# L1 cross attention and L2 attention in a new order, and wide FFNs rounded by ScalarE to int16 and transposed by DMA

## The chip, the cores and the metric

The kernel runs on one core of one Trainium2 chip. The time is the device time of one execution in microseconds. One program computes a whole decoder stack of twelve sublayers for eight sequences.

## The reference, cut to what matters

`x` is [8, 256, 256]. Four layers follow one another, each with self attention, cross attention and an FFN, and after every sublayer comes `x = layernorm(x + sublayer(x))`. The change touches five of the twelve:

```python
# L1 cross attention: 16 heads of 16, context of 64 tokens
q = qdq(x) @ qdq(wq).T + bq        # qdq: s = max|row|/127, round(x/s) clipped to +-127, times s
attn = softmax(q @ k.T / 4)
out = qdq(attn @ v) @ qdq(wp).T + bp
# L1, L2, L3 FFN: 256 -> 1024 -> 256, ternary weights, activations rounded per token
xq = round(x * 127 / max|x|)       # L1F: x and hidden are first RMS-normed and multiplied by g
h = silu(xq @ w1.T) * (xq @ w2.T)  # L2F: with biases; L3F: 128 levels, h goes through a Walsh-Hadamard transform
out = quant(h) @ w3.T
# L2 attention: linear attention with decay, 16 heads of 16, chunks of 128
scores = (q @ k.T) * decay_mask    # per head and chunk
intra = scores @ v;  inter = (q * q_decay) @ kv
out = rms_norm(intra + inter) @ wo
```

## The kernel before, in words

Each sublayer is a function that opens one or more blocks. In a block every engine has a program of its own, and semaphores order them. The sublayers follow one another with a barrier between them. They are called L0A, L0X, L0F, L1A, L1X and so on (layer; A attention, X cross attention, F FFN), and the names of their tiles begin with that. `x` stays in SBUF as `X`, 128 rows by two tiles a sequence. `v(...)` issues a VectorE instruction and lets VectorE wait until it has finished, unless `free=True` is given. The weights of the next sublayer are loaded during the one before, by the queue of SP (`prefetch`). All matmuls on attention data are float32, those of the wide FFNs bfloat16 on whole numbers.

**L1X** (`sublayer_l1_cross`) takes a sequence in U = 4 steps u (two tiles of 128 rows, two groups of 8 heads). In a step TensorE makes `scores(u + 1)` (one matmul of 512 columns), `turn(u - 1)` (four transposes of the probabilities) and `values(u - 2)`; VectorE takes the maxima and differences (L1818, L1821), ScalarE the exponential (L1803) and the copy of the turned tile (L1797). The rest of a sequence hangs on the step's number r = u % 4. On VectorE: r = 0 the next sequence's input is quantized (`quantize_rows`: maximum, scale, reciprocal, two multiply-and-add-magic (L1625), two subtract-and-scale (L1627)); r = 1 the outputs of the sequence before are divided and quantized; r = 2 the queries get bias and scale (`vec_q`, L1648); r = 3 the residual, the statistics, a wait for GpSimd's power -1/2, and the scaling. On TensorE: r = 1 turns the quantized input, r = 2 turns the outputs and makes the next queries, r = 3 projects. The last sequence's projection has a block of its own (`last_rows`).

**The wide FFNs** (`sublayer_ternary_ffn`; L1F with norms, L2F with biases, L3F with the Hadamard transform) take 16 tiles of 128 rows, one a step s, in a software pipeline. VectorE in step s: `quantize_input(s)`, `quantize_hidden(s - 3)`, `norm(s - 4)`, the two halves of `gate_times_up(s - 1)`, in L3F `across_chunks(s - 1)` (six additions), and `scale_and_add(s)` (the maximum and scale of the hidden tile s - 2, the residual and statistics of tile s - 3). ScalarE: silu of the gates of tile s - 1, the copy of the turned hidden tile, the copy of the turned input, and last the multiplication by the reciprocal scale with the rounding constant added (L1430). TensorE: the gates of s - 1, eight transposes of the rounded hidden tile s - 3 (L1354), its down projection into the same bank, the transposes of the input s. In L3F eight transposes and eight matmuls of the transform stand between them.

**L2A** (`sublayer_l2_attn`) takes a sequence in U = 8 steps of two heads; the heads lie 32 rows apart in the array (`at`), and the output of `values` lies in 32 columns of it. In step u TensorE makes `scores(u + 1)` (four matmuls of 128 columns, all with the row group of u), `values(u - 2)`, and a piece of the work around it: r = 0 turns x, r = 1, 2 queries and keys, r = 2, 3 the output projection, r = 4 values, r = 5, 6, 7 turned pieces and the keys' product. VectorE multiplies the scores by the decay (`decay`, L2583) and rotates (L2351). The tile `sd` has three buffers.

**L0A** and **L0X** aren't changed, but they contain the same operations: L0A makes its scores by turns over two row groups (L492) and its values over four column groups (L520); L0X has DMA transposes issued by SP (L810) and a VectorE conversion from int16 to bfloat16 (L925).

## Time and profile before

| | us |
|---|---|
| three runs | 3930.85, 3927.05, 3930.51 |
| median | 3930.51 |
| the profiled execution, its own time | 3925.62 |
| its span, first to last instruction | 3923.8 |

Over the span TensorE is busy 3158.0 us (80%), VectorE 2699.9 (69%), ScalarE 1818.9 (46%), GpSimd 467.4 (12%). Such shares are a mean over twelve stages with different limits; which engine bounds a stage is read from a window of that stage. Busy time of TensorE also grows when its clock is granted at half speed, so the granted clock has to be read beside it.

### The profile page before, as it was taken

How to read it: one execution, taken by the hardware profiler on the slowest of the kernel's cores; microseconds unless marked ns; L12 is line 12 of the kernel's file. 1: busy time of each engine (PE TensorE's matmuls, PEld its weight loads, DVE VectorE, ACT ScalarE, POOL GpSimd, SP SyncE). 2: the span in 40 equal slices, each digit the busy share in tenths (PEclk: the TensorE clock that was granted, in tenths of full speed). 3: DMA queues.
4: the chain of work that ended last, by engine and by line, in shares of the span. 5: the costliest groups of instructions: out<-in, count | busy, mean ns of one | idle time of the engine just before them, and what ended most of it. 6: DMA issues, size and time to landing. Idle time of an engine off the chain costs nothing. (4 is left out here: it accounts for less than half of the span.)

```text
span 3923.8 us, 55642 instructions
## 1 busy us (share of the span) xinstructions
PE 3158.0 (80%) x17296; PEld 2305.3 (59%) x17296; DVE 2699.9 (69%) x8364; ACT 1818.9 (46%) x5598; POOL 467.4 (12%) x585
## 2 busy tenths in 40 slices
PE   7975555979999997765599974579999999999565
PEld 5653334747777776542277762247777777777354
DVE  4668885278788885668844468856666666666597
ACT  4547673145555552225411123346666666666243
POOL 0012110011111110111101110011111111111100
PEclk9995556989999998765599996689999999999588
DMA  1005554000000001000000012000000000000000
GB/s 58 1 24 95 102 103 129 1 14 1 1 1 1 1 1 41 1 31 1 16 1 1 1 45 105 1 11 1 1 1 1 1 1 1 1 1 1 33 1 22
DMA packets 141731, 83.68 MB, mean 21 GB/s; under 512 B 135424, under 2 KB 139648, under 8 KB 139776
## 3 DMA queue, kind: packets, MB, share of 16 engines
q1 hardware_dynamic: 141440, 80.14, 7.8%
q8 instruction: 142, 2.33, 0.2%
q14 instruction: 149, 1.22, 0.1%
HBM read 44.47 MB, written 2.10 MB: 12 GB/s over the span
## 5 line engine op out<-in xcount | busy, mean ns | idle before, releaser
L2219 DVE CUSTOM_DVE_ANT_0 L3A_masked<-ps,L3A_hidden,L3A_negrstd 128x128 f32<-128x128 f32 (+1 forms) x512 | 193.6, 416 | 321.9 <-PE ps L2110 232.7
L2168 ACT ACTIVATE L3A_probs<-L3A_masked,L3A_negmax 128x128 f32<-128x128 f32 (+1 forms) x512 | 228.7, 449 | 237.3 <-DVE L3A_negmax L2219 237.2
L336 PE MATMUL ps<-s_weights_b,s_XT 128*128 128x512 f32 (+1 forms) x640 | 299.6, 597 | 30.0 <-ACT L1A_qn L2026 8.3
L2138 PE MATMUL ps<-s_weights_b,L3A_OT 128*128 128x256 f32 x1024 | 264.2, 381 | 14.5 <-DVE s_R L2248 14.5
L336 PE MATMUL ps<-s_weights_b,s_Xc 128*128 128x512 f32 x512 | 243.6, 598 | 7.5 <-DVE L3A_rot L2083 3.3
L2091 POOL TENSOR_TENSOR L3A_rstd<-L3A_ve,s_mhalf 128x4 f32<-128x4 f32 x144 | 145.0, 1007 | 849.7 <-DVE L3A_ve L2051 849.7
L885 ACT ACTIVATE L0X_pf<-ps,L0X_bias,L0X_qscale 128x512 int16<-128x512 f32 x256 | 197.0, 777 | 90.8 <-DVE L0X_bias L918 90.2
L336 PEld LDWEIGHTS ps<-s_weights_b,s_XT 128*128 128x128 f32 x640 | 121.8, 209 | 121.7 <-issue 72.3
L2138 PEld LDWEIGHTS ps<-s_weights_b,L3A_OT 128*128 128x128 f32 x1024 | 175.1, 191 | 28.8 <-issue 15.6
L915 DVE TENSOR_REDUCE L0X_negmax<-ps 128x2 f32<-128x1024 f32 x128 | 156.1, 1220 | 35.5 <-PE ps L826 35.0
L2168 ACT ACTIVATE L1A_probs<-L1A_masked,L1A_negmax 128x128 f32<-128x128 f32 (+1 forms) x256 | 114.3, 447 | 120.2 <-DVE L1A_negmax L2219 117.5
L2016 ACT ACTIVATE s_oT<-ps 128x128 bf16<-128x128 f32 x576 | 150.8, 277 | 22.5 <-PE ps L336 22.5
L320 POOL TENSOR_TENSOR s_rs<-s_ve,s_mhalf 128x2 f32<-128x2 f32 x74 | 55.3, 747 | 874.2 <-DVE s_ve L264 874.2
L2110 PE MATMUL ps<-L3A_kT,L3A_qT 128*128 128x256 f32 x512 | 154.3, 383 | 0.0
L2127 PE MATMUL ps<-L3A_probsT,L3A_V 128*128 128x256 f32 x512 | 152.5, 380 | 0.0
L2091 POOL TENSOR_TENSOR L1A_rstd<-L1A_var,s_mhalf 128x4 f32<-128x4 f32 x80 | 82.5, 1031 | 562.1 <-DVE L1A_var L2046 562.1
L2138 PE MATMUL ps<-s_weights_b,L1A_OT 128*128 128x256 f32 x512 | 131.9, 380 | 8.9 <-DVE s_R L2248 8.9
L336 PE MATMUL ps<-s_XT,s_weights_a 128*128 128x256 f32 (+1 forms) x512 | 124.7, 397 | 12.5 <-ACT s_XT L205 5.4
L2127 PEld LDWEIGHTS ps<-L3A_probsT,L3A_V 128*128 128x128 f32 x512 | 89.1, 190 | 72.2 <-issue 72.1
L336 PEld LDWEIGHTS ps<-s_weights_b,s_Xc 128*128 128x128 f32 x512 | 87.4, 191 | 74.5 <-issue 63.0
L2003 ACT COPY L3A_qT<-ps 128x512 f32<-128x512 f32 x128 | 75.1, 587 | 117.9 <-PE ps L1987 117.9
L546 ACT ACTIVATE L0A_probs<-ps,L0A_negmax 128x128 f32<-128x128 f32 (+1 forms) x256 | 86.6, 422 | 90.8 <-DVE L0A_negmax L581 90.0
(512 smaller groups left out, 8650.6 us busy)
## 6 DMA issues: line engine op xcount, KB each, us to landing
s_weights_b<-w_L3A SPq DMA_DIRECT2D x1, 9984.0 KB, 27.0
s_weights_b<-w_L1A SPq DMA_DIRECT2D x1, 7936.0 KB, 21.4
s_weights_a<-w_L2F SPq DMA_DIRECT2D x1, 4224.0 KB, 12.3
s_weights_b<-w_L1F SPq DMA_DIRECT2D x1, 3840.0 KB, 11.9
s_weights_b<-w_L3F SPq DMA_DIRECT2D x1, 3136.0 KB, 11.1
s_weights_a<-w_L2A SPq DMA_DIRECT2D x1, 2898.0 KB, 9.8
s_weights_a<-w_L0F SPq DMA_DIRECT2D x1, 2176.0 KB, 9.0
s_X<-x SPq DMA_DIRECT2D x1, 2048.0 KB, 8.3
```

What stands on the lines that cost most here:

```text
L336: last = pe.matmul(out, lhs(k), rhs(k), start=(k == 0), stop=(k == n - 1))
L546: last = a.activation(pr[:, p % 4, x, cols], c.bank(2 * (p % 2) + x)[:, cols], ACT.Exp, bias=nmx[:, p % 4, j, x:x + 1])
L885: last = a.activation(pf[:, p % 3, x, :], c.bank(2 * (p % 3) + x), ACT.Exp, scale=qs[:, b % 2, at:at + 1], bias=nms[:, p % 4, x:x + 1], ac ...
L915: v(eng.tensor_reduce(nmx[:, p % 4, :], c.ps[:, 2 * (p % 3):2 * (p % 3) + 2, :], AX.X, ALU.max, negate=True))
L2003: a.copy(dst[:, 2 * b:2 * b + 2, :].rearrange("p h t -> p (h t)"), c.bank(2)).then_inc(side_taken, 1)
L2016: last = a.activation(squares[:, j, s * P:(s + 1) * P], c.bank(j)[:, s * P:(s + 1) * P], ACT.Square, accum_out=var[:, j, s:s + 1])
L2091: p.tensor_tensor(rstd[:, j, 4 * slot(g):4 * slot(g) + 4], src[:, j, :], c.mhalf[:, 0:4], ALU.pow).then_inc(pow_ready, 1)
L2110: pe.matmul(bank[:, P:3 * P], qT[:, g % 2, s, P:TOK], kT[:, i % 2, h // REP, :], start=True, stop=True).then_inc(scores_made, 1)
L2127: pe.matmul(c.bank(7)[:, 0:TOK], V[:, i % 2, 0, d], prT[:, u % 2, 0:TOK], start=True, stop=False)
L2138: last = pe.matmul(c.bank(3)[:, j * DM:(j + 1) * DM], OT[:, u % 4, j * P:(j + 1) * P], w["wo"][:, h, :], start=(h == 0 and j == 0), stop=( ...
L2168: last = a.activation(pr[:, u % 4, cols], ms[:, u % 2, cols], ACT.Exp, bias=nmx[:, h, j:j + 1], scale=-1.0, accum_out=sm[:, h, j:j + 1])
L2219: last = eng.tensor_tensor_reduce(out=ms[:, u % 2, cols], in0=s[:, cols], in1=hidden[:, P - j * P:2 * P], scale=-1.0 if gated else nrs[:, ...
```

## The change

**L1X.** Both roundings (of the inputs and of the outputs) go to ScalarE as two activations each: multiply and write int16, multiply again and write float32. VectorE keeps maximum, scale and reciprocal (`row_scales`). ScalarE also makes the queries' bias and scale. GpSimd adds the projection's bias to x. The inputs are rounded and turned a sequence ahead, outputs are turned at r = 3 and projected at r = 0 of the sequence after the next, the residual is at r = 2 and its scaling at r = 0 after that. The loop has two more rounds, and the block of the last projection goes.

**L2A.** Two heads make a pair; their scores are issued by turns, and so are their values; the pieces of other work stand between and after. `sd` has four buffers, and VectorE does two decays in a row.

**The wide FFNs.** ScalarE multiplies and writes int16, both for the inputs (`round_input`) and for the hidden tile. The hidden tile is transposed by a DMA from SP's queue, and then converted to bfloat16: in L1F and L2F by ScalarE, in L3F by VectorE (`clip_hidden`). TensorE's eight transposes and the copy out of PSUM go. VectorE's order within a step changes: `norm`, the gates, `quantize_input` (now one conversion), across, clip, `scale_input(s + 1)`, `scale_and_add`. The down projection is one step later (LAG = 4). In L1F the factor of the RMS norm is applied to the scales and not to the rows.

```diff
+    LAG = 4
...
+            @block.sync
+            def _(sp):
+                for t in range(NT):
+                    sp.wait_ge(hround_ready, t + 1)
+                    if t >= 2:
+                        sp.wait_ge(hiT_ready, t - 1)
+                    sp.dma_start_transpose(out=hqT[:, t % 2, :].rearrange("p (c q) -> p c q", q=P), in_=hq[:, t % 2, :]).then_inc(
+                        hq_turned[t % 2], 16)
...
-                for s in range(NT + 3):
+                for s in range(NT + LAG):
                     if 1 <= s <= NT:
                         gates(s - 1, 0)
                         gates(s - 1, 1)
                     if hadamard and 2 <= s < NT + 2:
                         turn_hidden(s - 2)
-                    if s >= 3:
-                        turn_quantized(s - 3)
                     if hadamard and 2 <= s < NT + 2:
                         transform(s - 2)
-                    if s >= 3:
-                        down(s - 3)
+                    if s >= LAG:
+                        down(s - LAG)
...
+                def round_input(t):
+                    a.wait_ge(xscale_ready, t + 1)
+                    if t >= 2:
+                        a.wait_ge(xi_ready, t - 1)
+                    for q in range(XQ):
+                        x = qx[:, q, :] if norms else row(t)
+                        last = a.activation(xq[:, t % 2, q, :], x, ACT.Copy, scale=rq[:, t, q:q + 1])
+                    last.then_inc(xround_ready, 1)
...
+                    if s < NT:
+                        round_input(s)
                     if 1 <= s <= NT and not biases:
                         silu(s - 1, 0)
...
-                    if s >= 3:
-                        a.wait_ge(hi_turned, s - 2)
-                        a.copy(hiT[:, (s - 3) % 2, :], c.bank(7, BF16)).then_inc(hiT_ready, 1)
...
+                    if s >= 3 and not hadamard:
+                        t = s - 3
+                        a.wait_ge(hq_turned[t % 2], 16 * (t // 2 + 1))
+                        if t >= 2:
+                            a.wait_ge(y_tile, t - 1)
+                        a.copy(hiT[:, t % 2, :], hqT[:, t % 2, :]).then_inc(hiT_ready, 1)
...
-                        a.activation(qh[:], x, ACT.Identity, bias=c.magic[:, 0:1],
-                                     scale=rc[:, s - 2, 2:3]).then_inc(hround_ready, 1)
+                        if s >= 4:
+                            a.wait_ge(hq_turned[s % 2], 16 * (s // 2 - 1))
+                        a.activation(hq[:, s % 2, :], x, ACT.Copy, scale=rq[:, s - 2, 2:3]).then_inc(hround_ready, 1)
...
+                def scale_input(t):
+
+                    last = XQ - 1
+                    if norms:
+                        if t:
+                            eng.wait_ge(xround_ready, t)
+                        for q in range(XQ):
+                            v(eng.tensor_tensor(qx[:, q, :], row(t), w["g1" if q == 0 else "g2"], ALU.mult), free=q < last)
+                        v(eng.tensor_reduce(am[:, t, 0:XQ], qx[:], AX.X, ALU.max, apply_absolute_value=True))
+                        eng.wait_ge(xrr_ready, t + 1)
+                        v(eng.tensor_scalar(am[:, t, 0:XQ], am[:, t, 0:XQ], rr[:, t, 0:1], least, ALU.mult, ALU.max))
+                        v(eng.tensor_scalar(am2[:, t, 0:XQ], am[:, t, 0:XQ], 1.0 / levels, None, ALU.mult))
+                    else:
+                        v(eng.tensor_reduce(am[:, t, 0:1], row(t), AX.X, ALU.max, apply_absolute_value=True))
+                        v(eng.tensor_scalar(am2[:, t, 0:XQ], am[:, t, 0:XQ], least, 1.0 / levels, ALU.max, ALU.mult))
+                    v(eng.reciprocal(rc[:, t, 0:XQ], am2[:, t, 0:XQ]), None if norms else xscale_ready, free=not norms)
+                    if norms:
+                        v(eng.tensor_scalar(rq[:, t, 0:XQ], rc[:, t, 0:XQ], rr[:, t, 0:1], None, ALU.mult), xscale_ready, free=True)
+                    b_ = am2[:, t, 0:XQ] if norms else am2[:, t, 0:1].to_broadcast([P, 2])
+                    v(eng.tensor_tensor(f[:, t, 0:2], b_, wsc[:, 0:2], ALU.mult))
...
+                    eng.wait_ge(xround_ready, t + 1)
...
+                    x = xq[:, t % 2].rearrange("p q d -> p (q d)")
+                    o = xi[:, t % 2].rearrange("p q d -> p (q d)")
+                    v(eng.tensor_scalar(o, x, levels - 1.0 if hadamard else levels, None, ALU.min), xi_ready, free=True)
...
+                def clip_hidden(t):
+                    eng.wait_ge(hq_turned[t % 2], 16 * (t // 2 + 1))
                     if t >= 2:
-                        eng.wait_ge(hi_turned, t - 1)
-                    whole(v, hi[:, t % 2, :], qh[:], hi_ready)
+                        eng.wait_ge(y_tile, t - 1)
+                    v(eng.tensor_scalar(hiT[:, t % 2, :], hqT[:, t % 2, :], levels - 1.0, None, ALU.min), hiT_ready, free=True)
...
-                for s in range(NT + 4):
+                scale_input(0)
+                for s in range(NT + LAG + 1):
                     if norms and 2 <= s < NT + 2:
                         hidden_mean(s - 2)
-                    if s < NT:
-                        quantize_input(s)
-                    if 3 <= s < NT + 3:
-                        quantize_hidden(s - 3)
-                    if s >= 4:
-                        norm(s - 4)
+                    if s > LAG:
+                        norm(s - LAG - 1)
+                    if norms and s + 1 < NT:
+                        input_mean(s + 1)
                     if 1 <= s <= NT:
                         for hf in range(NH):
                             gate_times_up(s - 1, hf)
-                        if hadamard:
-                            across_chunks(s - 1)
-                    if norms and s + 1 < NT:
-                        input_mean(s + 1)
+                    if s < NT:
+                        quantize_input(s)
+                    if hadamard and 1 <= s <= NT:
+                        across_chunks(s - 1)
+                    if hadamard and 3 <= s < NT + 3:
+                        clip_hidden(s - 3)
+                    if s + 1 < NT:
+                        scale_input(s + 1)
...
+        def row_scales(v, out, x, sem):
+
+            e = v.eng
+            v(e.tensor_reduce(am[:], x, AX.X, ALU.max, apply_absolute_value=True))
+            v(e.tensor_scalar(out[:, 0, :], am[:], 1.0 / 127.0, 1e-8, ALU.mult, ALU.max))
+            v(e.reciprocal(out[:, 1, :], out[:, 0, :]), sem, free=True)
+
+        def act_quantize(a, out, x, whole, scales, rounded, first, ready):
+
+            for k in range(TT):
+                a.activation(whole[:, k, :], x[:, k, :], ACT.Copy, scale=scales[:, 1, k:k + 1]).then_inc(rounded, 1)
+            for k in range(TT):
+                a.wait_ge(rounded, first + k + 1)
+                a.activation(out[:, k, :], whole[:, k, :], ACT.Copy, scale=scales[:, 0, k:k + 1]).then_inc(ready, 1)
...
+        def act_q(a, b, t=0):
+            a.wait_ge(q_made, t + 1)
             for ch in range(KC):
-                v(v.eng.tensor_scalar(qT[:, b, ch, :], c.bank(0)[:, ch * TOK:(ch + 1) * TOK], w["bq"][:, ch:ch + 1],
-                                      DH ** -0.5, ALU.add, ALU.mult), q_ready)
+                a.activation(qT[:, b, ch, :], c.bank(0)[:, ch * TOK:(ch + 1) * TOK], ACT.Identity, bias=bqs[:, ch:ch + 1],
+                             scale=DH ** -0.5).then_inc(q_ready, 1)
...
+                for u in range((NS + 2) * U):
                     b, r = u // U, u % U
                     if u + 1 < NS * U:
                         scores(u + 1)
                     if 1 <= u <= NS * U:
                         turn(u - 1)
-                    if u >= 2:
+                    if 2 <= u < NS * U + 2:
                         values(u - 2)
-                    if b == NS:
-                        continue
-                    if r == 1:
+                    if r == 0 and b + 1 < NS:
                         pe_turn_xq(pe, b)
-                    if r == 2:
-                        if b:
-                            pe.wait_ge(S.on_ready, TT * b)
-                        S.pe_turn_on(pe, 6)
+                    if r == 0 and b >= 2:
+                        project_outputs(b - 2)
+                    if r == 1 and b + 1 < NS:
                         pe_q(pe, b)
-                    if r == 3:
-                        S.pe_project_on(pe, wpT, 7, b)
+                    if r == 3 and 1 <= b <= NS:
+                        turn_outputs(b - 1)
...
+                for u in range((NS + 2) * U):
                     b, r = u // U, u % U
                     if u < NS * U:
                         a.wait_ge(diff_ready, u + 1)
                         a.activation(pr[:, u % 2, :], pr[:, u % 2, :], ACT.Exp).then_inc(exp_ready, 1)
-                    if u >= 1:
+                    if 1 <= u <= NS * U:
                         take(u - 1)
-                    if b < NS and r == 1:
+                    if r == 0 and b + 1 < NS:
+                        if b:
+                            a.wait_ge(q_made, b)
                         S.act_xT(a, t=b)
-                    if b < NS and r == 2:
-                        S.act_oT(a, 6, b)
+                    if r == 1 and b + 1 < NS:
+                        act_q(a, (b + 1) % 2, b)
+                    if r == 2 and 1 <= b <= NS:
+                        act_on(a, b - 1)
+                    if r == 3 and b + 2 < NS:
+                        act_xq(a, b + 2, b + 1)
+                    if r == 3 and 1 <= b <= NS:
+                        if b > 1:
+                            a.wait_ge(S.y_made, b - 1)
+                        S.act_oT(a, 6, b - 1)
...
+                def residual(i):
+                    eng.wait_ge(S.y_made, i + 1)
+                    eng.wait_ge(xb_ready, i + 1)
+                    v(eng.tensor_tensor(c.R[:], Xb[:], c.bank(7).rearrange("p (j d) -> p j d", j=TT), ALU.add), S.y_read)
+                    S.vec_norm_stats(v)
+
+                row_scales(v, xs, c.X[:, 2 * TT:3 * TT, :], x_scaled)
+                for u in range((NS + 2) * U + 1):
                     b, r = u // U, u % U
                     if u < NS * U:
                         differences(u)
-                    if b and r == 1:
+                    if r == 0 and b >= 3:
+                        S.vec_norm_scale(v, b - 2, b - 3)
+                    if r == 1 and 1 <= b <= NS:
                         outputs(b - 1)
-                    if b == NS:
-                        continue
-                    if r == 0:
-                        quantize_rows(v, Xq, c.X[:, bass.ds((b + 2) * TT, TT), :], xq_ready)
-                    if r == 2:
-                        vec_q(v, (b + 1) % 2, b)
-                    if r == 3:
-                        S.vec_add_y(v, b, 7, w["bp"], b)
-                        S.vec_norm_stats(v)
-                        S.vec_norm_scale(v, b, b)
+                    if r == 2 and b >= 2:
+                        residual(b - 2)
+                    if r == 3 and b + 2 < NS:
+                        eng.wait_ge(xq_ready, TT * (b + 1))
+                        row_scales(v, xs, c.X[:, (b + 3) * TT:(b + 4) * TT, :], x_scaled)
...
+                        g.tensor_tensor(Xb[:], c.X[:, (b - 1) * TT:b * TT, :], over(w["bp"], TT), ALU.add).then_inc(xb_ready, 1)
+                        S.pool_rstd(g, b - 2)
...
+                def scores(p):
+                    b = 2 * p // U
+                    if b and 2 * p % U == 0:
                         pe.wait_ge(turned_ready, 5 * b - 1)
-                    if u >= 2:
-                        pe.wait_ge(sd_ready, u - 1)
-                    at, chunks = heads(u)
-                    for x, ch in enumerate(chunks):
+                    if p:
+                        pe.wait_ge(sd_ready, 2 * p)
+                    for x in range(2):
                         for j in range(TT):
                             t = slice(j * P, (j + 1) * P)
-                            last = pe.matmul(c.bank(4 + u % 2)[:, x * TOK + j * P:x * TOK + (j + 1) * P], qT[at, b % 2, 1, ch, t],
-                                             qT[at, b % 2, 0, ch, t], start=True, stop=True)
-                    last.then_inc(scores_made, 1)
-
-                def values(u):
+                            for u in (2 * p, 2 * p + 1):
+                                at, chunks = heads(u)
+                                last = pe.matmul(c.bank(4 + u % 2)[:, x * TOK + j * P:x * TOK + (j + 1) * P], qT[at, b % 2, 1, chunks[x], t],
+                                                 qT[at, b % 2, 0, chunks[x], t], start=True, stop=True)
+                                if x == j == 1:
+                                    last.then_inc(scores_made, 1)
...
+                            for u in (2 * p, 2 * p + 1):
+                                at, _ = heads(u)
+                                d = slice(ch * P + at.start, ch * P + at.stop)
+                                last = pe.matmul(bank[at, x * TOK + j * P:x * TOK + (j + 1) * P], V[:, b % 2, j, d], sd[:, u % 4, x, j, :],
+                                                 start=False, stop=(x == j == 1))
+                                if x == j == 1:
+                                    last.then_inc(o_made, 1)
...
+                for p in range(NS * U // 2 + 1):
+                    b, r = 2 * p // U, 2 * p % U
+                    if b < NS:
+                        scores(p)
+                        side(b, r)
+                    if p:
+                        values(p - 1)
+                    if b < NS:
+                        side(b, r + 1)
...
-                    decay(u)
+                    if u % 2 == 0:
+                        decay(u)
+                        decay(u + 1)
```

## Rows read from the trace of the kernel before

**Rows 1.** Busy time by window: L1X, L2A, one tile of L1F.
```profile
core 0: us, PE busy (x) PEld busy (x) DVE busy (x) ACT busy (x) POOL busy (x), PEclk, DMA share, GB/s
...
1553.00:1748.00 195.00, 147.73 (x650) 111.08 (x648) 127.44 (x298) 44.47 (x81) 22.32 (x29) 0.75 0.00 1
...
1974.00:2256.00 282.00, 274.81 (x1724) 215.94 (x1722) 119.49 (x352) 48.22 (x96) 27.31 (x32) 0.96 0.00 1
...
1824.20:1834.84 10.64, 6.94 (x28) 3.36 (x28) 10.01 (x27) 5.43 (x9) 1.59 (x3) 0.50 0.00 0
```

**Rows 2.** Tile view of L1X_pr: the differences of the 32 steps.
```profile
L1821 DVE TENSOR_TENSOR L1X_pr<-ps,L1X_mx x32: 690/692/692, 1553.1 to 1730.0; 128x512 f32<-128x512 f32 x32
```

**Rows 3.** Timeline of L1X, TensorE: start, duration (us), idle before.
```profile
1644.24 2.07 PE L1745 MATMUL ps<-L1X_kd,L1X_qT 128*128 128x512 f32 x2 [4.15 <-DVE L1X_pr L1821]
...
1658.76 1.12 PE L1745 MATMUL ps<-L1X_kd,L1X_qT 128*128 128x512 f32 x2 [1.10 <-DVE L1X_qT L1648]
...
1660.97 1.97 PE L336 MATMUL ps<-L1X_wpT,s_oT 128*128 128x256 f32 x8
1662.78 1.02 PE L1745 MATMUL ps<-L1X_kd,L1X_qT 128*128 128x512 f32 x2
```

**Rows 4.** Timeline of L1X, VectorE.
```profile
1648.76 0.26 DVE L1829 RECIPROCAL L1X_ri<-ps 128x16 f32<-128x16 f32 x1 [0.82 <-PE ps L1766]
...
1651.52 0.62 DVE L1625 TENSOR_SCALAR L1X_tmp<-s_R,L1X_inv 128x256 f32<-128x256 f32 x2
...
1657.70 1.00 DVE L1648 TENSOR_SCALAR L1X_qT<-ps,s_weights_a 128x256 f32<-128x256 f32 x2 [3.46 <-PE ps L336]
```

**Rows 5.** Timeline of L2A, TensorE.
```profile
2101.02 1.15 PE L2493 MATMUL ps<-L2A_qT 32*128 32x128 f32 x8
2102.11 1.06 PE L2514 MATMUL ps<-L2A_sd,L2A_V 128*32 128x128 f32 x8
2103.10 1.09 PE L2384 MATMUL ps<-s_const,L2A_rp 128*128 128x128 f32 x8
```

**Rows 6.** Timeline of L0A, TensorE.
```profile
151.03 0.92 PE L492 MATMUL ps<-L0A_kT,L0A_qT 32*128 32x128 f32 x8
151.89 0.40 PE L496 MATMUL ps<-s_causal_bf,s_idb 128*128 128x128 bf16 x4
...
155.09 0.86 PE L520 MATMUL ps<-L0A_probsT,L0A_V 128*32 128x256 f32 x16
155.88 0.92 PE L492 MATMUL ps<-L0A_kT,L0A_qT 32*128 32x128 f32 x8
```

**Rows 7.** Tile views of the rounded hidden tiles of L1F, L2F, L3F (min/median/max ns).
```profile
L1298 DVE TENSOR_SCALAR L1F_hi<-L1F_qh x16: 693/694/705, 1791.9 to 1943.2; 128x1024 bf16<-128x1024 f32 x16
...
L1298 DVE TENSOR_SCALAR L2F_hi<-L2F_qh x16: 693/694/695, 2397.3 to 2557.2; 128x1024 bf16<-128x1024 f32 x16
...
L1298 DVE TENSOR_SCALAR L3F_hi<-L3F_qh x16: 693/694/696, 3743.0 to 3907.8; 128x1024 bf16<-128x1024 f32 x16
```

**Rows 8.** Timeline of one tile of L3F, VectorE.
```profile
3808.05 0.42 DVE L1455 TENSOR_REDUCE L3F_am<-s_X 128x1 f32<-128x256 f32 x1
...
3808.95 0.35 DVE L1461 TENSOR_SCALAR L3F_qx<-s_X,L3F_rc 128x256 f32<-128x256 f32 x1
...
3810.85 1.54 DVE L1479 SCALAR_TENSOR_TENSOR L3F_h<-ps,L3F_f,L3F_gt 128x512 f32<-128x512 f32 x2
...
3818.58 0.16 DVE L1525 RECIPROCAL L3F_rc<-L3F_am 128x1 f32<-128x1 f32 x1
...
3819.24 0.42 DVE L1455 TENSOR_REDUCE L3F_am<-s_X 128x1 f32<-128x256 f32 x1
```

**Rows 9.** Timeline of the same tile of L3F, ScalarE.
```profile
3818.84 1.20 ACT L1430 ACTIVATE L3F_qh<-ps,s_magic,L3F_rc 128x1024 f32<-128x1024 f32 x1 [4.22 <-DVE L3F_f L1526]
3819.94 1.26 ACT L1394 ACTIVATE L3F_gt<-ps,L3F_f 128x512 f32<-128x512 f32 x2
```

**Rows 10.** DMA issues by line, KB each, us to landing.
```profile
L0X_pT<-L0X_ph SPq DMA_TRANSPOSE x128, 3.1
```

**Rows 11.** Groups by form in L0X, VectorE.
```profile
L925 DVE CAST L0X_ph<-L0X_pf 128x1024 bf16<-128x1024 int16 x70 | 30.5, 435 | 0.2
```

184 lines of the change are left out of this document (93 added, 91 removed).

## The prediction

> **What bounds the kernel now.** The times come first: three runs with a median of 3930.5 us, and a profiled execution of 3925.6 us whose span is 3923.8 us. The sum below is made against 3925.6; the median lies 4.9 us above it, and the last number adds that. The kernel is twelve stages, one after another, so what a stage gains the whole gains. The second view is therefore busy time by stage [rows 1]. The reader is to see three different limits. In L2A (1974 to 2256) TensorE is busy 274.81 of 282.00 us: it is the bound. In the wide FFNs VectorE is: in the 10.64 us of one tile of L1F it is busy 10.01, with TensorE at a granted clock of 0.50. In L1X (1553 to 1748) nothing is: TensorE is busy 147.73 of 195.00 us at a clock of 0.75, VectorE 127.44. There a chain between engines sets the pace.
>
> The third view is each stage's rhythm. In L1X 32 steps begin from 1553.1 to 1730.0, which makes 22.8 us for a sequence of four [rows 2]. In its timeline TensorE begins a step's scores only after 4.15 us of waiting for VectorE, and then runs them in 2.07 us; the same two matmuls take 1.12 us where the clock is full [rows 3]. So the chain costs twice: in waits, and in the clock that falls after them.
>
> **L1X, part by part.** (1) VectorE loses two pairs of quantizing instructions, 0.62 us for the first instruction group of a pair and as much again for the second, so about 2.6 us a sequence; the queries' bias and scale, 1.00 us; and one bias addition of about 0.7 us [rows 4]. Its 127.44 us are 15.9 a sequence, 11.5 afterwards. ScalarE takes eight roundings and two query activations, which it does in its idle time: it was far below half busy. GpSimd adds the residual's bias, about 1 us, ahead of its power. (2) The order. Before, VectorE at r = 3 does the whole of "add y, statistics, wait for GpSimd, scale", and the next differences stand behind it: that is what the 4.15 us are. After, the scaling is a sequence later, the turn and projection of the outputs too, and the inputs are rounded a sequence ahead. (3) What TensorE has to do is the same. At full clock a step of scores, turn and values takes 1658.76 to 1660.97 = 2.21 us and a projection 1660.97 to 1662.78 = 1.81 [rows 3]; four steps, two projections and two groups of four transposes (about 0.45 each, my estimate from the step's own four) make 8.8 + 3.6 + 0.9 = 13.4 us a sequence. That is the floor. (4) What it still waits for: at r = 1 VectorE waits for the last values, then does outputs and row scales (1648.76 to 1651.52 = 2.76 us [rows 4]), then differences, about 1.4, then ScalarE's exponential, 0.6: 4.8 us, against about 4.0 of TensorE's own work in that time (queries 1.8, a step 2.2). That leaves 0.8. ScalarE's rounding of the next inputs at r = 3 stands between two exponentials, and the transposes of r = 0 wait for it, about 1.3. So 13.4 + 2.1 = 15.5 us at full clock. The floor of the cost is 14.2 (half of these waits hidden by queues), its top 20.0: at the present clock of 0.75 the work is 13.4 / 0.75 = 17.9, plus 2.1. I take 15.5, because TensorE would then work 13.4 of 15.5 us, and L2A, as densely busy, is the stage with the high clock [rows 1, 5]. 22.8 - 15.5 = 7.3, times 8 = 58; two more rounds of the loop at the end, where one short stage goes, cost about 3: **-55 us**.
>
> **L2A.** The removed form issues the four score matmuls of one head, which all use one group of 32 rows of the array, then the next head's. The new one alternates between two heads, and so between two row groups and two banks; the values alternate between two groups of 32 output columns. L0A already does this, and it shows the price. Four alternating matmuls there (8 records, two for each float32 matmul), 768 columns in all, take 151.03 to 151.89 = 0.86 us [rows 6], where L2A's four, 512 columns, take 2101.02 to 2102.11 = 1.09 [rows 5]. With a fixed part F and a cost c for a column, F + 512c = 1.09 and, if two run at a time, F + 768c/2 = 0.86: c = 1.8 ns, F = 0.17. A pair of heads (1024 columns, two at a time) is then 0.17 + 0.92 = 1.09: two heads for the price of one. The values say the same: 155.09 to 155.88 = 0.79 us for 1536 columns four at a time, against 0.99 for 512 columns now (2102.11 to 2103.10), and a pair would be about 1.0. That is 1.09 + 0.99 = 2.08 us saved in each of four pairs, 8.3 a sequence. Against it stand: 0.4, because a pair has twice L0A's weight loads in that time; a wait of 2.0 at r = 0, because turning the next x needs a copy that VectorE now does behind two heads' decays (0.76 each, then 0.42), where it stood behind one, and TensorE has nothing else queued; 0.3 at r = 5, where the pieces wait for the variance. A wait of 0.7 for the turned pieces goes, as a turn and the keys' product now stand between. 8.3 - 0.4 - 2.3 + 0.7 = 6.3, times 8: **-50 us**. Bounds: 7.0 without the loads' share (-56), 3.5 if the waits are double (-28).
>
> The row is that two heads cost as one [rows 5, 6]. The Trainium skill (TensorEngine Tiling (Array Packing), Key Properties) says that tiles run independently and that a change of tiling mode drains the engine; by its up to four times for 32 rows the stage could gain more, but only two groups alternate here, so the sum would be the same. The trace agrees with the drain in that a fixed part of 0.17 us is left over.
>
> **The three FFNs of 1024 columns.** Sixteen tiles each. A full tile takes 10.64 us in L1F [rows 1] and 11.19 in L3F (3808.05 to 3819.24 [rows 8]); in L2F fifteen intervals from 2397.3 to 2557.2 give 10.66, the last of them lighter, so about 10.8 for a full one [rows 7]. The rounding that goes away on VectorE is 0.694 us there. The new chain is: ScalarE rounds to int16, the queue of SP transposes by DMA, and ScalarE (L1F, L2F) or VectorE (L3F) converts to bf16; the eight TensorE transposes and their PSUM copy go. The same DMA transpose of 128x1024 two-byte elements runs in L0X: 3.1 us from issue to landing, 128 of them [rows 10]. The same conversion runs there too: 0.435 us for 1024 elements [rows 11]. The transposed tile is wanted 3.3 us or more after the rounding in L1F and L2F and 6.6 in L3F, so the DMA is hidden or nearly; a landing late by up to 2 us moves only a copy and not the gates. Then VectorE in L3F: it loses 0.39 + 0.33 + 0.73 and gains 0.15 + 0.36, and would come to 10.3.
>
> But the order moves too. Before, VectorE begins a tile with the input's and the hidden's quantizing, and only at 3810.85, 2.8 us after 3808.05, needs the gate's silu [rows 8]. After, only the norm stands there. ScalarE does the hidden's rounding first (1.10 us from 3818.84 to 3819.94), then the new rounding of the input (about 0.3), then silu (0.67, half of 1.26 and a fixed part) [rows 9]. So a ring closes: from the gate product to the hidden's scale is 3810.85 to 3818.74 = 7.89, plus the moved input scales 0.90 (3808.05 to 3808.95), plus 0.15 and 0.36 for the two conversions = 9.30; then 1.0 + 0.3 + 0.67 on ScalarE and 0.08 of semaphores: 11.35 us against 11.19. L3F gains nothing: +0.15 times 14 steady tiles, and about 1 for the DMA in the last tile: +3. In L1F the ring also holds the squares of the input and two roundings: by the same reckoning 8.1 + 2.8 = 10.9 against 10.64, +5 with its tail. In L2F silu is not first (the bias is added by VectorE before it), so the ring is not closed: VectorE's work of 9.8 decides, and -1.0 for 14 tiles and +1.4 in the tail make -12. Together **-4 us**. Bounds: -40 if VectorE has no gap in any (L1F 9.5, L3F 10.3), +15 if L3F's TensorE falls to the low clock (its work is then some 11.2 us a tile, as in the stage's first tiles) and the int16 conversions run at 0.69.
>
> The transposes' price is taken from the row, 3.1 us. The Trainium skill (DMA: Bandwidth & Descriptors, DMA Transpose (X-bar)) says that this way moves 261 GB/s; by that alone the 256 KB would need 1.0 us, and the sum would not change.
>
> **The sum.** 3925.6 - 55 - 50 - 4 = 3816.6, and 4.9 for the median: 3821 us.
>
> **The rivals.** (a) L1X's clock stays at 0.75: for it speaks that the clock fell after each wait of 4.15 us, and that waits remain; against it that they get short. Cadence 20.0, -19 instead of -55: 3857. (b) L2A's heads do not overlap, for example because the two groups of 128 columns are too short for it. Then only half of the fixed parts goes (0.32 for each of four pairs), 2.3 of waits come and 0.7 go: +3 instead of -50, 3874. L0A speaks against it. (c) The waits I added are hidden: L1X at 14.2 (-66), L2A -56, and ScalarE's ring opens in one or two FFNs (-24): 3784. (d) The other side: alternating costs a fixed part for every record of a matmul and not for every group. Each pair has 32 records; it decides from the point where a record pays 58 ns, for then 32 pairs lose 59 us and, with the 50 not gained, eat up the 109. At the full 0.17 they would lose 174 us: 3821 + 50 + 174 = 4045. In L0A four alternating matmuls with 8 records take 0.86 us in all, so it is nearly excluded.
>
> **How the numbers follow.** The forecast 0.50, (a) 0.17, (b) 0.11, (c) 0.18, (d) 0.03, and 0.01 that it all cancels. The forecast's own range is 3795 to 3845. The range that leaves out no more than 2 in 10 goes from (c)'s 3784 to beyond (b): 3780 to 3885. What this kernel's measurement can tell from no change is 0.2%, 8 us; within it I put 0.02, slower 0.03, faster 0.95.
>
> **What would show it.** L1X: 32 differences within about 125 us, TensorE's clock near 1, no wait of 4 us ahead of the scores. L2A: a group of 16 score records in 1.1 us, a wait of about 2 us before each turn of x, VectorE busier by share. L3F and L1F: an idle time of about 1.2 us before VectorE's gate product, released by ScalarE's silu; L2F without it and at 9.8 us a tile; SP's transposes at about 3.1 us each with nobody waiting long. The prediction is wrong if L1X's granted clock stays low, if the L2A pairs take 2.1 us, or if a wait for the DMA stands ahead of the gates.

## The result, and the profile after

The changed kernel takes 3808.64 us (median of 4 runs, 3804.77 to 3809.32) against 3928.78 us (4 runs), a ratio of 0.9696, 95% interval 0.9683 to 0.9708. That is 120 us less; the forecast was 3821, 109 less. The profiled execution has a span of 3803.0 us.

The stages follow one another, so each can be measured from the first instruction that only the next one issues (for L1F, L2F and L3F the weight sums `tot`, for L2A its first turned piece `rp`, for L3A its rotation; L1X begins at its first differences). L2A stands here with L2X, whose code did not change.

| stage | before, us | after, us | difference | forecast |
|---|---|---|---|---|
| L1X | 199.6 | 133.4 | -66 | -55 |
| L1F | 212.2 | 220.8 | +8.6 | +5 |
| L2A, L2X | 397.6 | 346.3 | -51.3 | -50 |
| L2F | 212.6 | 194.3 | -18.3 | -12 |
| L3A, L3X | 1129.6 | 1130.3 | +0.7 | 0 |
| L3F | 219.1 | 226.8 | +7.7 | +3 |

Up to L1X the changed execution was 2 us ahead, as two executions can be. Cut at L2X's first turn of x, L2A alone went from 319.0 to 264.3 us (-54.7), and L2X from 78.6 to 82.0: its unchanged instructions met a lower clock. The first reading is busy time by window, for L1X, L2A and one tile of L1F, as in [rows 1]:

```profile
core 0: us, PE busy (x) PEld busy (x) DVE busy (x) ACT busy (x) POOL busy (x), PEclk, DMA share, GB/s
1551.00:1684.50 133.50, 115.83 (x626) 87.52 (x624) 90.86 (x202) 71.21 (x151) 29.89 (x34) 0.92 0.00 1
1913.70:2137.00 223.30, 207.45 (x1695) 159.81 (x1696) 116.42 (x351) 47.10 (x94) 27.33 (x32) 0.93 0.00 1
1759.96:1771.37 11.41, 6.07 (x20) 2.40 (x20) 9.00 (x26) 6.17 (x12) 1.65 (x3) 0.50 0.12 24
```

In L1X the granted clock went from 0.75 to 0.92 and TensorE from 76% to 87% busy. In L2A the clock fell from 0.96 to 0.93 although the engine has less to do. In the tile of L1F VectorE has 1 us less work (10.01 to 9.00), and the tile is 0.8 us longer: work went and a wait came.

The tile view and the TensorE timeline of L1X after, which answer to [rows 2, 3]:

```profile
L1913 DVE TENSOR_TENSOR L1X_pr<-ps,L1X_mx x32: 690/691/693, 1551.1 to 1660.6; 128x512 f32<-128x512 f32 x32
```
```profile
1598.27 1.10 PE L1818 MATMUL ps<-L1X_kd,L1X_qT 128*128 128x512 f32 x2 [0.30 <-DVE L1X_pr L1913]
1599.41 0.63 PE L1827 MATMUL ps<-s_const,L1X_pr 128*128 128x128 f32 x4
1599.87 0.98 PE L1839 MATMUL ps<-L1X_Vd,L1X_pT 128*128 128x34 f32 x8
...
1601.78 1.13 PE L1818 MATMUL ps<-L1X_kd,L1X_qT 128*128 128x512 f32 x2 [0.21 <-DVE L1X_pr L1913]
```

The 31 intervals of the differences make 109.5 us, 14.1 for a sequence against 22.8. The wait of 4.15 us ahead of the scores is gone, 0.30 and 0.21 are left, and the scores take 1.10 us instead of 2.07: both halves of what the chain cost.

L2A, TensorE, at the turn of x, to be read against [rows 5]:

```profile
2021.18 1.07 PE L2621 MATMUL ps<-L2A_sd,L2A_V 128*32 128x128 f32 x16
2022.18 0.66 PE L2486 MATMUL ps<-s_const,L2A_qr 128*128 128x128 f32 x4
2022.67 1.06 PE L2500 MATMUL ps<-L2A_V,L2A_kr 128*128 128x128 f32 x8
2023.66 1.16 PE L2596 MATMUL ps<-L2A_qT 32*128 32x128 f32 x16
2026.71 0.93 PE L199 MATMUL ps<-s_const,s_Xc 128*128 128x128 f32 x4 [1.90 <-DVE s_Xc L2702]
2027.57 1.92 PE L2621 MATMUL ps<-L2A_sd,L2A_V 128*32 128x128 f32 x16
```

The values of two heads (16 records) take from 2021.18 to 2022.18 = 1.00 us, what one head took before. Then comes the wait for the copy of x, 1.90 us, and behind it the same 16 records take 1.92 instead of 1.07: TensorE runs at its lower level. The wait, 1.81 to 1.90 us, stands at the turn of x in all eight sequences; the clock is low behind seven of them, and at the turn of 2000.22 it stays full (values in 1.00).

Last the FFNs: VectorE, where each tile's gate products begin (L1F, then L3F), and ScalarE ahead of them (the same), as in [rows 8, 9]:

```profile
1759.96 1.54 DVE L1503 SCALAR_TENSOR_TENSOR L1F_h<-ps,L1F_f,L1F_gt 128x512 f32<-128x512 f32 x2 [1.24 <-ACT L1F_gt L1396]
1771.37 1.54 DVE L1503 SCALAR_TENSOR_TENSOR L1F_h<-ps,L1F_f,L1F_gt 128x512 f32<-128x512 f32 x2 [1.24 <-ACT L1F_gt L1396]
...
3696.96 1.53 DVE L1503 SCALAR_TENSOR_TENSOR L3F_h<-ps,L3F_f,L3F_gt 128x512 f32<-128x512 f32 x2 [0.65 <-ACT L3F_gt L1396]
3708.47 1.54 DVE L1503 SCALAR_TENSOR_TENSOR L3F_h<-ps,L3F_f,L3F_gt 128x512 f32<-128x512 f32 x2 [0.66 <-ACT L3F_gt L1396]
```
```profile
1768.32 1.15 ACT L1448 ACTIVATE L1F_hq<-L1F_qh,L1F_rq 128x1024 int16<-128x1024 f32 x1 [4.16 <-DVE L1F_rq L1555]
...
1769.77 0.89 ACT L1405 ACTIVATE L1F_xq<-L1F_qx,L1F_rq 128x256 int16<-128x256 f32 x2
1770.57 1.24 ACT L1396 ACTIVATE L1F_gt<-ps,L1F_f 128x512 f32<-128x512 f32 x2
...
3706.25 1.11 ACT L1448 ACTIVATE L3F_hq<-ps,L3F_rc 128x1024 int16<-128x1024 f32 x1 [4.44 <-DVE L3F_rc L1553]
3707.26 0.50 ACT L1405 ACTIVATE L3F_xq<-s_X,L3F_rc 128x256 int16<-128x256 f32 x1
3707.66 1.26 ACT L1396 ACTIVATE L3F_gt<-ps,L3F_f 128x512 f32<-128x512 f32 x2
```

A tile takes 11.41 us in L1F and 11.51 in L3F, and VectorE waits for ScalarE's silu ahead of the products: the ring of the forecast. In L2F it takes 2334.68 to 2344.46 = 9.78, without that wait. The transposes land after 3.0 to 3.1 us.

### The profile page after: what moved, and what is told of

Same layout as the page of the kernel before. It is cut to its first block and busy times, and to the rows that moved or that the text cites. A ratio compares the mean times of both kernels' runs of the same rounds, so it can differ in the third digit from the quotient of the medians.

```text
span 3803.0 us, 55008 instructions
## 1 busy us (share of the span) xinstructions
PE 3030.0 (80%) x16888; PEld 2200.9 (58%) x16888; DVE 2608.3 (69%) x8195; ACT 1856.9 (49%) x5724; POOL 475.3 (12%) x589
## 3 DMA queue, kind: packets, MB, share of 16 engines
q8 instruction: 139, 2.28, 0.2%
## 5 line engine op out<-in xcount | busy, mean ns | idle before, releaser
L2118 ACT ACTIVATE s_oT<-ps 128x128 bf16<-128x128 f32 x576 | 150.9, 277 | 23.5 <-PE ps L336 23.4
L320 POOL TENSOR_TENSOR s_rs<-s_ve,s_mhalf 128x2 f32<-128x2 f32 x73 | 54.7, 749 | 773.2 <-DVE s_ve L264 773.2
```

Of the source, the lines that this page charges most:

```text
L2118: last = a.activation(squares[:, j, s * P:(s + 1) * P], c.bank(j)[:, s * P:(s + 1) * P], ACT.Square, accum_out=var[:, j, s:s + 1])
```

## The experiments

All times are medians. E1 to E3 take one part of the change each into the kernel before (3929.5 us in the same job); E4 to E9 alter the changed kernel (3808.6), and E10 to E12 add up what helped.

**E1, E2, E3: the parts alone.** The whole of L1X, of L2A, of the three FFNs, in the kernel before.

> The kernel before with the new L1X alone. By the theory that each stage gains by itself, the whole gains what the L1X stage gained in the trace after: 1752.7 to 1684.5 at the start of L1F's first reduction, -68 us (about 3860). By the rival, that part of the gain came from a neighbour or from the clock of a later stage, it is -55 us or less.

> The kernel before with the new L2A alone. Theory: -51 us (about 3877), the difference of the two traces between L2A's first turned piece and L2F's first reduction. Rival: L2A profits from a TensorE clock that the new stages leave behind; then clearly less than -51.

> The kernel before with the new wide FFNs alone. Theory: L1F +9 and L3F +8 eat up L2F's -18: within 5 us of the kernel before. Rival: the new FFNs gain in all three, and the traces' boundaries only hide it: -20 us or more.

Measured: 3866.6 (-63), 3871.7 (-58) and 3929.0 (-0.5; ratio 0.9996, 0.9986 to 1.0005). They add up to -121 against the change's -120, so no part needs another. The third is no idle part: inside it L1F loses 8.7 us and L3F 7.6, and L2F gains 18.2. L2A alone gained more than in the table: L2A with L2X took 339.7 us at a mean clock of 0.94 there, and 346.3 at 0.91 in the changed kernel, with the same instructions. That is not because it stands alone: in E4, where the other parts stand beside it, the same stretch took 338.4 us at 0.94. In both, the low clock follows five of the eight waits at the turn of x, and in the changed kernel seven.

**E4: L1X's roundings back on VectorE, in the new order.**

```diff
-    act_xq(a, 0, 0) ... act_on(a, b - 1) ... act_xq(a, b + 2, b + 1)      # ScalarE
-    row_scales(v, xs, c.X[:, TT:2 * TT, :], x_scaled)
+    quantize_rows(v, Xq, c.X[:, TT:2 * TT, :], xq_ready)
-    row_scales(v, os_, Ob[:], o_scaled)
+    quantize_rows(v, c.On, Ob[:], S.on_ready)
```

> The kernel after, in which L1X keeps its new order but VectorE does both roundings again, as it did before (2.6 us more of VectorE a sequence, and 3.6 us less of ScalarE). If the new order is what took the stage from 22.8 to 15.1 us a sequence, it costs little: VectorE's work goes from 11.5 to 14.1 us, under the 15.1, and the outputs' rounding stands 1.3 us in front of the next differences: +5 to +15 us against the kernel after. If the move of the roundings to ScalarE is what did it, the stage goes back towards 22.8: +50 us.

Measured: 3816.2 (3815.3 to 3825.1), +7.6. By the two profiles the stage has 146.2 us against 133.4:

```profile
1555.80:1702.00 146.20, 117.25 (x624) 91.26 (x622) 113.03 (x259) 49.53 (x94) 29.92 (x34) 0.87 0.00 1
```

VectorE has 113.03 us of work instead of 90.86, which is 22 us more, and the stage lengthens by 13 in the profile and the whole by 8 in the medians. The two differ because L2A with L2X, which this edit does not touch, took 7.9 us less in this execution (see E2). So of the 66 us in L1X some 13 come with ScalarE's roundings and 53 with the rest of the new form. That rest is the order and two smaller moves, which E4 leaves in place: the queries' bias and scale on ScalarE and the projection's bias on GpSimd. Together they are the 14 us of work that VectorE still has less than before (113.03 against 127.44 [rows 1]). No run separates them from the order.

**E5: L2A in pairs of heads, but one head after the other.**

```diff
-    for x in range(2):
-        for j in range(TT):
-            for u in (2 * p, 2 * p + 1):
+    for u in (2 * p, 2 * p + 1):
+        for x in range(2):
+            for j in range(TT):                 # the same for values
```

> The kernel after, in which L2A still works in pairs of heads but issues one head's score matmuls and then the other's, and the values likewise; everything else is as after. If two alternating heads run at the same time in the array, a pair loses 1.09 + 1.00 us: 32 pairs, +60 to +68 us against the kernel after. If the gain came from the pairs' fewer changes of shape and the new order of the side work, it is +10 us at most.

Measured: 3843.5 (3834.4 to 3851.7), +35, between the two. TensorE's timeline:

```profile
2033.67 1.71 PE L2596 MATMUL ps<-L2A_qT 32*128 32x128 f32 x16
2035.31 1.09 PE L2486 MATMUL ps<-s_const,L2A_rp 128*128 128x128 f32 x8
2036.23 0.61 PE L2615 MATMUL ps<-L2A_qd,L2A_kv 128*128 128x128 f32 x4
2036.77 1.53 PE L2621 MATMUL ps<-L2A_sd,L2A_V 128*32 128x128 f32 x16
2038.23 0.66 PE L2486 MATMUL ps<-s_const,L2A_qr 128*128 128x128 f32 x4
```

The scores of a pair take 1.64 us: 2.18 as two separate heads [rows 5], 1.64 one behind the other, 1.09 alternating. The values: 1.98, 1.46, 1.00. So half of the gain comes from putting two heads next to each other, the other half from alternating. My expectation took the whole for the second.

The overlap explains both halves. Three stretches of 0.10 us inside that pair's scores, with the number of records of L2596 at work:

```profile
2034.05:2034.15 0.10, 0.10 (x3) 0.10 (x3) 1.00 0.00 0
2034.40:2034.50 0.10, 0.10 (x5) 0.10 (x6) 1.00 0.00 0
2035.00:2035.10 0.10, 0.10 (x3) 0.10 (x2) 1.00 0.00 0
```

TensorE has three matmul records at work in the first and the last, and five in between. Read record by record, the second head's first one begins 0.55 us after the first head's first one, when three of the first head's eight have not begun. In the changed kernel it begins 0.01 us after. So this run does not take the overlap of two heads away; it leaves about half of it.

**E6: the copy of the next x ahead of the two decays.**

```diff
+    if r == 0:
+        v(eng.tensor_copy(c.Xc[:], c.X[:, bass.ds((b + 2) * TT, TT), :]), S.x_copied)
     if u % 2 == 0:
         decay(u)
         decay(u + 1)
-    if r == 0:
-        v(eng.tensor_copy(...), S.x_copied)
```

> The kernel after, in which L2A's copy of the next x stands in front of the two decays of a sequence's first pair and not behind them. If the 1.90 us that TensorE waits ahead of each turn of x are VectorE's two decays and the copy, 8 of them go: -12 to -15 us against the kernel after. Rival: the wait only moves to the turned copy by ScalarE or to the decays: within 3 us.

Measured: 3790.8 (3785.5 to 3791.0), -18; the stage with L2X takes 322.8 us instead of 346.3.

```profile
2018.71 1.16 PE L2596 MATMUL ps<-L2A_qT 32*128 32x128 f32 x16
2020.10 0.66 PE L199 MATMUL ps<-s_const,s_Xc 128*128 128x128 f32 x4 [0.23 <-DVE s_Xc L2699]
2020.68 1.07 PE L2621 MATMUL ps<-L2A_sd,L2A_V 128*32 128x128 f32 x16
```
```profile
1918.30:2120.00 201.70, 199.34 (x1688) 155.27 (x1688) 116.32 (x349) 46.58 (x93) 27.33 (x32) 0.97 0.01 1
```

The wait fell from 1.90 to 0.23 us, which is 13 us over eight sequences. The rest, 5 by the medians and 10 by the profiles, is the clock: 0.97 instead of 0.93 in L2A, where the values behind the wait take 1.07 instead of 1.92 in all eight sequences, and 3 of the 10 us lie in L2X (78.9 us instead of 82.0).

**E7, E8: the ring of L1F and L3F.** E7 puts silu ahead of the hidden rounding on ScalarE (it then stands at the end of the step before). E8 also puts the norm behind the gate products on VectorE, in all three FFNs.

```diff
+    if s < NT and not biases:                   # E7
+        silu(s, 0)
+        silu(s, 1)
     if 2 <= s < NT + 2:
         a.wait_ge(hscale_ready, s - 1)
...
     if 1 <= s <= NT:                            # E8
         for hf in range(NH):
             gate_times_up(s - 1, hf)
+    if s > LAG:
+        norm(s - LAG - 1)
```

> The kernel after, in which ScalarE takes the silu of a tile's gates before it rounds the hidden tile two behind, and not after it (L1F and L3F). If the ring hidden scale, rounding, silu, gate product sets the pace, the idle 1.24 us (L1F) and 0.65 us (L3F) ahead of VectorE's gate product go, 14 or 15 times each: -24 to -28 us against the kernel after. If the ring is only a symptom and TensorE's late transform or the DMA holds the tile, little is gained: -10 us at most.

> As the run with silu first, and VectorE's norm (which waits for GpSimd's power, 0.54 to 0.73 us idle a tile in all three FFNs) stands behind the gate products. Theory: another 2.0 us a tile over the three, 15 tiles: -50 us against the kernel after in all. Rival: with VectorE gapless the transposing DMA or TensorE becomes the limit, and the second step gives under 10 us.

Measured: 3793.7 (-15, expected -24 to -28) and 3785.1 (-23.5, expected -50). The second step gave 8.6 us more, as its rival said (under 10). L1F went from 220.8 to 210.8 and 206.7 us; its tile took 10.20 in E7, nothing but VectorE's own work and 0.87 of waits. L2F went from 194.3 to 187.7 with the norm moved. So in L1F the ring is real. L3F, where as much was expected, gained 3.2 in E7 and no more in E8: 223.5. E8's trace says why:

```profile
3674.00 1.61 DVE L1503 SCALAR_TENSOR_TENSOR L3F_h<-ps,L3F_f,L3F_gt 128x512 f32<-128x512 f32 x2 [0.93 <-PE ps L336]
...
3685.14 1.61 DVE L1503 SCALAR_TENSOR_TENSOR L3F_h<-ps,L3F_f,L3F_gt 128x512 f32<-128x512 f32 x2 [0.69 <-PE ps L336]
```
```profile
3678.05 3.49 PE L1355 MATMUL ps<-s_weights_b,L3F_uT 128*128 128x128 f32 x16 [1.10 <-ACT L3F_uT L1417]
```

Behind the silu stood TensorE: the transform takes 3.49 us, the gates are late, and VectorE now waits for them. My expectation of L3F falls.

**E9: the down projection one tile earlier again.**

```diff
-    LAG = 4
+    LAG = 3
```

> The changed kernel with LAG = 3: the down projection follows in the same step in which the turned hidden tile is converted. Theory: the lag is worth nothing. In the changed kernel's trace TensorE has 2.1 to 4.4 us of idle time in each tile of L1F and L2F, so the projection can wait for ScalarE's conversion (done 3.4 us after the first gate product in L1F, 4.6 in L2F), run 1.2 to 1.9 us and still have the gates ready when VectorE wants them; in L3F the conversion of that tile ends before the transform does. One short step less at the end of each of three stages: -3 us against the changed kernel, 3801 to 3811. Rival: the lag hides the DMA. The projection, the input's transposes behind it on TensorE and the gates then stand behind the landing (3.0 us) and the conversion (1.0) in every tile, about 1 us a tile in L1F and L2F: +15 to +35, 3824 to 3844.

Measured: 3824.8 (3820.8 to 3827.1), +16: the rival's size, but not its mechanism. The stages lose 6.3 us in L1F, 6.9 in L2F and 3.3 in L3F. In L1F and L2F the steady tiles are as in the changed kernel (11.40 us; 9.79, as from 2329.32 to 2339.11), and the loss lies in the last tiles: 4.7 and 4.5 us of it behind the last gate product. VectorE's last two tiles of L1F:

```profile
1894.42 0.48 DVE L1540 SCALAR_TENSOR_TENSOR s_R<-ps,L1F_f,s_X 128x256 f32<-128x256 f32 x1 [3.17 <-PE ps L336]
...
1903.44 0.48 DVE L1540 SCALAR_TENSOR_TENSOR s_R<-ps,L1F_f,s_X 128x256 f32<-128x256 f32 x1 [5.76 <-PE ps L336]
```

With LAG = 4 the same two waits are 0.98 and 2.28 us. Where no other tile's work is left, rounding, landing (3.1), conversion (1.04) and projection (1.9) stand one behind another. With LAG = 3 the scale of the last tile also stands on VectorE behind the projection of the tile just before it, so two such chains follow one another. In L3F it is otherwise: behind the last gate product nothing is lost (38.2 us against 38.3), but three of the steady tiles take 12.42 us instead of 11.51. In them VectorE waits another 0.9 us for silu ahead of its second gate product; what makes silu late in these three and not in the others is not shown. That the lag is worth nothing is refuted; that it covers each tile's landing is refuted for L1F and L2F.

**E10: the three moves of E6 and E8 together. E11: E10 with L3F as it was before the change.**

> The changed kernel with all three moves that helped: the copy of the next x ahead of the decays in L2A (-18 alone), silu ahead of the hidden rounding and the norm behind the gate products (-23.5 alone, together). They touch different stages, and the stages follow one another, so they should add: 3808.6 - 18 - 23.5 = 3767 us, 3760 to 3774. If the clock of one stage depended on what ran in the one before, the sum would miss by more than 8 us.

> The kernel with all three moves, and L3F alone as it was before the change (VectorE rounds and clips, TensorE transposes). Reading: L3F took 219.1 us before, 226.8 in the changed kernel and 223.5 with silu and the norm moved, where TensorE's transform and transposes at the low clock now end VectorE's waits; so int16 and DMA transposes buy nothing in this stage: -4 us against the kernel with the three moves (-2 to -7). Rival: the old form was slow for its silu and order, and 223.5 against 219.1 is a matter of where the stage begins and ends: 0 or slower by up to 5 us.

Measured: 3761.4 (ratio 0.9576, 0.9563 to 0.9589) and 3757.5 (0.9568, 0.9555 to 0.9582). E10 is 47 us below the changed kernel where 41.5 were summed. E11 is another 4 below, within the scatter of both but as expected: in L3F the old form is no worse than the new one. Its tile takes 11.18 us with VectorE hardly idle (one gap of 0.17 us in two tiles), the new one's 11.4 on average with waits. Busy time in windows of 120 us of L3F, E11 first, then E10:

```profile
3598.00:3718.00 120.00, 80.65 (x529) 60.84 (x528) 112.76 (x256) 49.65 (x64) 5.95 (x11) 0.89 0.00 1
```
```profile
3593.00:3713.00 120.00, 84.52 (x449) 64.23 (x449) 101.81 (x238) 41.99 (x61) 5.43 (x10) 0.79 0.15 22
```

With 15% fewer instructions in the window TensorE is busy for longer, because its clock is 0.79 instead of 0.89. That called for the last run.

**E12: E10 with work for nobody on TensorE in L3F.**

```diff
     turn_hidden(s - 2)
+    for k in range(FCH):
+        pe.transpose(c.bank(0, BF16)[:, (4 + k % 4) * P:(5 + k % 4) * P], c.idb[:], c.idb[:])
     transform(s - 2)
```

> The kernel with all three moves, and in each tile of L3F eight bfloat16 transposes of a constant on TensorE between the turn of the hidden tile and the transform, where it waits 1.10 us for ScalarE's copy. Their result is read by nobody; the eight transposes that the DMA took over stood near this place before. Theory: L3F's granted clock fell from 0.89 to 0.79 because TensorE lost that work; the transform then takes 3.2 to 3.8 us instead of 2.05 and the gates come late for VectorE. With the filling the clock comes back to 0.86 or more, the transform falls toward 2.05, and a tile takes 10.3 to 10.9 us instead of 11.4: -7 to -15 us against the kernel with the three moves (3761), 3746 to 3754. Rival: the clock has another cause, or the eight change nothing in it. They fit into a wait, so the time stays within 3 us of 3761; at the low clock they take 0.9 of the 1.10 and may add up to 0.3 a tile.

Measured: 3741.9 (3740.2 to 3742.8; ratio 0.9526, 0.9513 to 0.9539), -19.5 against E10, which ran in another job against the same kernel before (3926.7 there, 3927.8 here). That is more than expected. It is the fastest version found. L3F takes 205.6 us instead of 224.3.

```profile
3632.06 1.85 PE L1347 MATMUL ps<-s_const,L3F_hb 128*128 128x128 f32 x8 [1.93 <-ACT L3F_hq L1450]
3633.70 1.06 PE L1375 MATMUL ps<-s_idb 128*128 128x128 bf16 x8
3635.01 2.31 PE L1355 MATMUL ps<-s_weights_b,L3F_uT 128*128 128x128 f32 x16 [0.25 <-ACT L3F_uT L1419]
```
```profile
3593.00:3713.00 120.00, 82.75 (x570) 65.85 (x580) 111.58 (x262) 46.96 (x67) 6.50 (x12) 0.89 0.20 25
```

The clock is back at 0.89, the transform takes 2.31 us here (2.05 to 2.92 over the tiles, 3.3 to 3.8 in E10 from the second on), VectorE waits nowhere in a steady tile, and a tile takes 3671.78 to 3681.99 = 10.21 us. The eight transposes only change what TensorE does in a wait.

## Why the prediction was right, and where it was off

**The sum, 3821 forecast, 3808.6 measured.** The parts missed by -11 (L1X), +4 (L1F), -1 (L2A), -6 (L2F) and +5 us (L3F). That the whole came within 12 us of the forecast is in part luck, as the FFNs' errors have both signs.

**L1X, -55 forecast, -66 measured.** The mechanism is as predicted, and E4 shows that the roundings are the smaller part of it; how much of the larger part is the order alone is not shown. The cadence was nearly right, but out of two wrong terms. Busy time in one steady sequence of the changed kernel:

```profile
1594.09:1609.20 15.11, 14.32 (x81) 10.59 (x81) 11.48 (x27) 9.33 (x20) 4.33 (x5) 1.00 0.00 0
```

A sequence takes 15.11 us (VectorE's outputs begin at 1594.09 and 1609.20), near the forecast's 15.5. TensorE is busy 14.32 of them at full clock, where the forecast's work term had 13.4, so that term was 0.9 too small. A step behind a wait takes 2.65 us and not 2.21 (1598.27 to 1600.92). And it is idle 0.8, where the term of the waits had 2.1. The two errors nearly cancel, and that is luck. Some 8 us more come from outside the steady part: by the differences the first two sequences, where nothing is projected yet, take 8.6 and 12.2 us, so that the mean is 14.1. The two added rounds cost 1.3 us, from the last difference to the next stage, not 3. The rival that the clock stays at 0.75 fell.

**L2A, -50 forecast, -51 measured with L2X**, a right sum with some luck in it: L2A alone gained 54.7 us and L2X, which stood in no term, lost 3.4. That a pair costs as one head is exact (1.09 and 1.00 us), and the wait of 2.0 us at the turn of x is there with 1.9, eight times. Not in the forecast was what follows the wait: slow matmuls, in L2A and in L2X, worth 5 to 10 us in E6. E2 and E4, where the clock stood 0.03 higher, show a like size for a part of them, 6.6 and 7.9 us. The two terms of the overlap hold. In E5 a head's eight score records begin 0.112 us apart, which is 1.74 ns a column, and a head's 1.09 us leave 0.19 as the fixed part; I had 1.8 and 0.17 [rows 5, 6]. With 1.74 and 0.19 L0A's four matmuls, 768 columns two at a time, come to 0.86 us, as measured. The rival "heads do not overlap" is excluded, by the 1.09 us of a pair and by E5, where two heads overlap even one behind the other. Its price of 53 us stays untested, as E5 (35 us) left about half of the overlap.

**L2F, -12 forecast, -18 measured.** The tile is 9.8 us as forecast. The tile before was mis-sized: its full tiles alternate between 10.8 and 11.2 us (VectorE waits 0.46 to 0.88 for silu in them), 11.0 in the mean and not 10.8. Between the first gate product and the last, eleven full tiles gave 12.4 us, the first three 3.4 (26.3 to 22.9) and the last 1.2. The two ends beyond gave another 1.4, where I had put a loss of 1.4.

**L1F and L3F, +5 and +3 forecast, +8.6 and +7.7 measured.** The ring is right, and E7 opened it. In L3F its VectorE part is 3696.96 to 3706.25 = 9.29 us, forecast 9.30. Mis-sized is ScalarE's part, 2.2 us (3706.25 to the gate product at 3708.47) instead of 2.05: the rounding of 128x256 to int16 takes 0.50 us alone and moves the next instruction by 0.40, where I had put 0.3. In L1F, with two of them, it is 3.05 instead of 2.8, and the part before it 8.36 instead of 8.1, together 11.41 where 10.9 stood. L3F's other miss is its end: 38.3 us from the last gate product instead of 35.4, 2.8 more where I had put 1. The Trainium skill (ScalarE: Activation LUTs, What ACT_TABLE_LOAD costs) gives 186 ns, 0.833 ns an element and 93 ns for a scale that is read from memory, and says that instructions back to back overlap by 93: an estimate of 0.49 us, and 0.40 to the next. The trace agrees with it (0.50 and 0.40), and my 0.3 had no row behind it.

**The bound that I left aside.** The forecast had as an upper bound that "L3F's TensorE falls to the low clock". It fell, from 0.89 to 0.78 over 120 us of the stage, and did not show in the tile because the silu ring was longer still. E7 and E8 uncovered it and E12 removed it. It was not the rounding on ScalarE alone that made L3F slow, but two rings, one behind the other.

**The DMA** was hidden in the steady tiles, as forecast (ScalarE waits 0.8 to 1.0 us for a landing in L1F, and nobody waits for ScalarE there). At the end of L1F and L2F it is not: E9. The 261 GB/s that the forecast quotes from the Trainium skill stand on that page under "Latency and other measured facts", for a non-contiguous middle dimension; no run here tests them, and the landing took 3.0 to 3.1 us.

**What stays open:** why in E5 the second head begins 0.55 us after the first and not earlier or later, why the low clock follows some of the 1.9 us waits and not others, and how L1X's 53 us divide between the order and the two smaller moves off VectorE.

## What to carry to other kernels

When work is moved off the engine that bounds a stage, write out the ring through the engine that takes it, in its queue order: what was placed ahead of the bound engine's input costs its full length each round, and one swap (silu first, the copy first) gave back 15 and 18 us here. After each such fix read the wait again; the next ring may stand right behind it. And count TensorE's clock as part of the price of taking work away from it: a short wait or a lighter tile can cost more through the clock than the work did.

## What the runs showed of the hardware

- Eight bfloat16 transposes that nobody reads, placed in a wait, raised the granted clock in L3F from 0.79 to 0.89 and saved 19.5 us, more than any other single move after the change.
- A 1.9 us wait in an otherwise dense stage was followed in seven of eight sequences by matmuls at the 1.2 GHz level (1.92 us for what takes 1.07 at 2.4 GHz); with 0.23 us in its place they stayed fast in all eight.
- Two heads of float32 matmuls, four of 128 columns each, on two row groups: 2.18 us apart, 1.64 one behind the other, 1.09 alternating. Even one behind the other, the second head begins 0.55 us after the first, before the first has issued its last records.
